# Row-block stores as two transfers of 64 partitions each, in a third-order interaction kernel

## The reference

```python
B, NF, D = 2048, 64, 128          # F: [B, NF, D], W: [NF, NF, D], K_w, Q_w: [D, D], float32
Kf  = einsum('bjd,ed->bje', F, K_w)
S   = einsum('bid,bjd->bij', F, Kf)
out = einsum('bij,ijd->bid', S, W)
out = out + einsum('bid,ed->bie', F, Q_w)
```

## Time and profile before

| what | value |
|---|---|
| median of 3 runs | 606.57 us (606.23 to 607.12) |
| the profiled execution | 606.42 us |
| its span in the trace | 604.6 us |
| TensorE busy | 596.4 us (99%) |
| VectorE busy | 399.2 us (66%) |
| ScalarE busy | 401.5 us (66%) |
| SP's DMA queue (q1) | 20736 packets, 75.83 MB, 31.8% of 16 engines |
| ACT's DMA queue (q10) | 8640 packets, 61.15 MB, 28.4% of 16 engines |
| granted TensorE clock, mean | 0.998 |

### The profile page before, as it was taken

How to read it: one execution, slowest core, us unless ns; L and a number is a source line. 1 busy time by engine, 2 the same in 40 slices (tenths; PEclk the granted TensorE clock), 3 DMA queues, 4 the chain that set the end, 5 groups by cost and what they waited for, 6 DMA issues and landing times.

```text
span 604.6 us, 17904 instructions
## 1 busy us (share of the span) xinstructions
PE 596.4 (99%) x7690; PEld 526.3 (87%) x7690; DVE 399.2 (66%) x412; ACT 401.5 (66%) x696; POOL 0.2 (0%) x4
## 2 busy tenths in 40 slices
PE   9999999999999999999999999999999999999995
PEld 7888989889898898988989898898988989889895
DVE  6556768567685675947749475685756768567486
ACT  7888393874938659295692947939387493865920
POOL 0000000000000000000000000000000000000000
PEclk9999999999999999999999999999999999999999
DMA  8644847457575575755657566484754857557177
GB/s 338 262 141 160 330 165 282 183 185 305 191 281 172 210 266 208 279 196 210 242 192 287 203 238 249 143 319 174 277 209 173 318 179 284 173 209 273 70 281 279
DMA packets 29452, 138.12 MB, mean 228 GB/s; under 512 B 3264, under 2 KB 3776, under 8 KB 21312
## 3 DMA queue, kind: packets, MB, share of 16 engines
q1 hardware_dynamic: 20736, 75.83, 31.8%
q10 hardware_dynamic: 8640, 61.15, 28.4%
HBM read 69.86 MB, written 67.11 MB: 227 GB/s over the span
## 4 chain that ended last, share of the span: by engine, by line
PE 98%; DVE 1%; issue 1%; DVEq 0%
PE ps L509 20%; PE ps L447 20%; PE ps L449 19%; PE ps L448 19%; PE ps L541 18%; DVE o_sb L372 1%; PE ps L576 1%; DVEq L49 0%; DVE o_sb L382 0%; PE ps L467 0%; PE ps L465 0%; PE ps L469 0%; DVE f_hi L388 0%; DVEq L115 0%
## 5 line engine op out<-in xcount | busy, mean ns | idle before, releaser
L337 DVE TENSOR_TENSOR f_lo<-f_ring,f_hi 128x1024 fp32r<-128x1024 f32 x124 | 151.8, 1224 | 168.2 <-ACT f_hi L217 166.6
L231 ACT ACTIVATE q_out<-ps 128x512 f32<-128x512 f32 x256 | 156.9, 613 | 6.6 <-PE ps L449 0.2
L222 ACT ACTIVATE kf<-ps 128x512 f32<-128x512 f32 x256 | 155.8, 609 | 3.5
L372 DVE TENSOR_TENSOR o_sb<-ps,q_out 128x1024 f32<-128x1024 f32 x127 | 145.1, 1215 | 19.4 <-PE ps L541 19.3
L240 ACT ACTIVATE s_t<-ps 128x512 f32<-128x512 f32 x32 | 19.1, 598 | 175.8 <-PE ps L509 175.8
L509 PE MATMUL ps<-f_ring,kf 128*64 128x64 f32 x4096 | 123.5, 222 | 0.3 <-issue 0.3
L509 PEld LDWEIGHTS ps<-f_ring,kf 128*64 128x64 f32 x4096 | 121.1, 138 | 2.6 <-issue 0.8
L541 PEld LDWEIGHTS ps<-s_t,w_sb 64*128 64x128 f32 x2048 | 115.6, 188 | 5.6 <-issue 5.6
L541 PE MATMUL ps<-s_t,w_sb 64*128 64x128 f32 x2048 | 118.6, 274 | 0.0
L447 PE MATMUL ps<-f_hi,k_hi 128*128 128x512 f32 x255 | 101.0, 396 | 0.0
L447 PE MATMUL ps<-f_hi,q_hi 128*128 128x512 f32 x256 | 100.0, 391 | 0.0
(11 more groups left out here) (39 smaller groups left out, 160.3 us busy)
## 6 DMA issues: line engine op xcount, KB each, us to landing
out<-o_sb SPq DMA_DIRECT2D x127, 512.0 KB, 3.5
f_ring<-f_t ACTq DMA_DIRECT2D x58, 1024.0 KB, 4.8
f_ring<-f_t SPq DMA_DIRECT2D x4, 1024.0 KB, 10.6
f_ring<-f SPq DMA_DIRECT2D x8, 256.0 KB, 5.3
w_sb<-w SPq DMA_DIRECT2D x1, 2048.0 KB, 17.8
out<-o_sb SPq DMA_DIRECT2D x2, 256.0 KB, 2.6
o_sb<-first SPq DMA_DIRECT2D x1, 192.0 KB, 2.9
o_sb<-first ACTq DMA_DIRECT2D x1, 192.0 KB, 3.4
```

What stands on the lines that cost most here:

```text
L222: nc.scalar.activation(kf[:, c // 2, c % 2 * CK:(c % 2 + 1) * CK, :, :].rearrange("d k h i -> d (k h i)"), ps[:, 2 * c % 8, :], COPY).then ...
L231: nc.scalar.activation(q_out[:, t % 2, :, :].rearrange("d i (h b) -> d i h b", h=2)[:, :, :, at:at + CK], q_bank(t * CHUNKS + c).rearrange ...
L337: nc.vector.tensor_tensor(f_lo[:, v % SPLIT, :], f_unit(v), f_hi[:, v % SPLIT, :].bitcast(F32), ALU.subtract).then_inc(flo_done, 1)
L372: nc.vector.tensor_tensor(o_sb[:, n % OBUF, :, :, :].rearrange("d x s b -> d s x b"), ps[:, bank:bank + 2, :].rearrange("d s (x b) -> d s ...
```

## The change

Each store of tiles 0 to 14 is issued as two DMAs, the first of partitions 0 to 63 and the second of partitions 64 to 127, one behind the other on SP's queue. The rows keep their 4 KB. Both raise the same semaphore by 16, so a slot's count rises by 32 for each such store, and the new function `stored(slot, n)` gives the count that all the slot's stores before n have brought; the three places that wait on `o_stored` use it. The stores of the last tile are as they were.

```diff
+        def stored(slot, n):
+            last = (TILES - 1) * UNITS
+            return sum(16 if b >= last else 32 for b in range(slot, n, OBUF))
...
             def store(t, k):
                 n = t * UNITS + k
                 sp.wait_ge(out_done, n + 1)
-                sp.dma_start(out[t, k, :, :],
-                             o_sb[:, n % OBUF, :, :, :].rearrange("d x s b -> d (x s b)")).then_inc(o_stored[n % OBUF], 16)
+                src = o_sb[:, n % OBUF, :, :, :].rearrange("d x s b -> d (x s b)")
+                if t == TILES - 1:
+                    sp.dma_start(out[t, k, :, :], src).then_inc(o_stored[n % OBUF], 16)
+                    return
+
+                for part in (slice(0, D // 2), slice(D // 2, D)):
+                    sp.dma_start(out[t, k, part, :], src[part, :]).then_inc(o_stored[n % OBUF], 16)
...
             for n in range(OBUF):
-                uses = len(range(n, TILES * UNITS, OBUF)) + (1 if n == slot else 0)
-                sp.wait_ge(o_stored[n], 16 * uses)
+                sp.wait_ge(o_stored[n], stored(n, TILES * UNITS) + (16 if n == slot else 0))
...
-                again = 1 if n - OBUF == (TILES - 1) * UNITS else 0
-                wait(dve, o_stored[n % OBUF], (n // OBUF + again) * 16)
+                again = 16 if n - OBUF == (TILES - 1) * UNITS else 0
+                wait(dve, o_stored[n % OBUF], stored(n % OBUF, n) + again)
...
-            dve.wait_ge(o_stored[n % OBUF], n // OBUF * 16)
+            dve.wait_ge(o_stored[n % OBUF], stored(n % OBUF, n))
```

## The result

The changed kernel takes 613.36 us in the median of six runs (611.62 to 618.0), the kernel before 606.73 us, now in six runs too (606.03 to 607.28). The ratio is 1.0113, 95% interval 1.0096 to 1.013: slower by 1.1%, near the forecast of 612.8 and inside its range. The runs now spread over 6 us where those of before spread over one.

What follows compares the result with a forecast made beforehand. TensorE, busy 99% of the span, was taken to bound the kernel, the DMA engines its end; 2.1 us of tile stalls plus 4.3 at the end, 6.4 on 606.4, gave 612.8 us, range 606.0 to 620.0.

Steps and rivals of the forecast that it cites:

- The deciding term: Stores of tiles 0 to 14: 16 engines share the way into 64 partitions, so a packet takes up to twice as long.
- The bounds 1.31 and 2.62: Time of a store on all 16 engines in us: 1.31 if unchanged, 2.62 if two engines on one way halve the pace.
- The pace T: Time one 512 KB store takes of all 16 DMA engines: 1.31 us before, 2.55 us forecast after the change.
- partners that fall out of step: Engines sharing a way but reading different halves don't slow each other; this kept the forecast at 2.55, just below 2.62.
- the formula 3T - 7.5: Stall per tile when late sum 7 delays chunk 2 of the projection: sum 2.3 us late against 2.2 slack, from T = 2.5 up.
- 14 waits of 0.15: TensorE's waits ahead of chunk 2 in the projections behind the stores of tiles 0 to 13, 2.1 us in all.
- 8T - 16.1: Delay of the kernel's end as tile 14's longer burst pushes back tile 15's stores: 4.3 us at T = 2.55.
- SP's issues: 120 more DMA instructions of 332 ns on SP; two per store, 0.66 us, fit within 1.14 us between sums: cost 0.
- More packets: 160 packets per store instead of 144, one closing packet more per engine: 0.05 us taken, 0 to 0.16 bounds, hidden.
- The loads: Load issued at 294.3 beside the longer store burst lands 2.6 us later; cast 1.3 us late, cost 0, 1.6 us left.
- the 9 us that I had named: Sign of being wrong: the load at 294.3 landing over 9 us after its issue.
- the prediction's reason against a faster kernel: Rival of a gain by another packet order: no wait on the page could be taken away; chance 0.03.

Runs made afterwards that it cites:

- The stores alone: Kernels without loads and compute issuing only the 128 stores from a constant tile: whole 175.66 us, halves 254.54, even and odd 177.25, both transfers from partitions 0 to 63 339.01.
- its move: Changed kernel with 32 more empty waits on TensorE in tile 1's projection: 620.11 us; gap moved from behind matmul 146 to behind 138 or 137.
- four issues: Changed kernel with each store of tiles 0 to 14 as four transfers of every fourth partition: 637.16 us, ratio 1.0514.

## Why the prediction was right, and where it was not

**The direction and its cause: shown.** The deciding term was where the rows are read from. Stores that read only partitions 0 to 63 take twice as long (2.56 us against 1.29), and even and odd partitions undo it. That pairs of engines share one way in is the reading that fits; no row shows which engine uses which way. The bounds 1.31 and 2.62 were the right ones. The Trainium skill's rule ("SBUF — State Buffer", "Door 1: The DMA port swizzle"), that partitions 0 to 63 reach only half of the ports, agrees with these runs: 205 GB/s from one half, 406 from all. The Trainium skill's statement on the same page ("Can I just issue two DMAs to hit both halves?") that two such transfers gain only 6% doesn't hold for a queue that alternates: 276 against 205 GB/s, a gain of 35%.

**The pace T: mis-sized.** I took 2.55, near the upper bound. The stores alone have 1.90, the burst in the kernel about 1.8 to 1.9 after a start at 191 GB/s, which is T = 2.7. The reason that I gave for staying below 2.62, partners that fall out of step, would be far stronger than I allowed. In the burst's first 1.5 us a 4 KB packet takes 311 ns in the median, afterwards 159, as before the change. That most packets are back at full pace is shown; that it is because their partners are in the other half is argued, from the kernel whose two halves are the same and which stays at 205.

**The tile: mechanism right, price wrong, and a second mechanism missed.** By the formula 3T - 7.5 a T of 1.90 stalls nothing. Yet at the start of the burst, where the stores stand that sums 6 and 7 wait for, the pace is 2.7, and sum 7 came 1.2 to 2.7 us late (3.2 in the first tile), for 2.3 forecast. Where it was 2.65 or more, chunk 2 waited, in four projections, 0.5 us each. These 1.9 us are near the 2.1 that I had as 14 waits of 0.15, by luck. What I had missed is TensorE's own instructions. They come as 16 KB packets through the same DMA engines; I had read that packet only as something that delays stores, and not asked who waits for the packet. In the changed kernel it starts up to 1.1 us later in the stage than the 1.5 us of before, and the gap follows. Over tiles 1 to 14 the scores stages are 6.7 us longer than before, and the projections from tile 1 on 3.8, together 10.5 of the 11.6 us of that execution; I had 2.1. Of what the 14 scores stages last above 7.62, 6.0 us lie in the ten with a late restart, and 1.5 in the four others, mostly in waits for sums; the kernel before had 0.8 of such excess. That the gap is a matter of the instruction stream is shown by its move. That a late packet is its cause rests on the 41 restarts that keep their distance from the packet's end; it leaves little room for another cause, but no run changed the packet alone.

**The end: right formula, wrong T.** 8T - 16.1 with 1.9 is below zero, and the end was not delayed to speak of: from the start of tile 14's rows to the end it takes 31.5 us (584.66 to 616.2) against 31.0, and these 0.5 us are the late restart in the last scores. The stretches show the engines at 0.38 in the microsecond from 603, so tile 14's burst is over just ahead of tile 15's first store:

```profile
591.00:603.00 12.00, 11.66 (x302) 10.79 (x299) 7.77 (x11) 5.78 (x11) 0.00 (x0) 1.00 0.85 280
603.00:604.00 1.00, 1.00 (x23) 1.00 (x21) 0.98 (x3) 0.00 (x0) 0.00 (x0) 1.00 0.38 135
```

I had 4.3 us there. **So the sum was right by luck, by two errors that offset each other**: 4.3 too much at the end, and too little in the tiles. A further 0.6 us of the profiled execution lie in the first projection, ahead of any store, and are no work of the change.

**SP's issues: mis-sized, and the cover was not there.** 332 ns is the price of an issue over 128 partitions that stands alone. Over half of them the first of a tile as a rule takes 466 to 472 ns, though it follows nothing, and one behind another some 600; split by columns, over 128 partitions, the first takes 332 and the second about 450. So both the transfer's form and the one before it count. With even and odd partitions two issues and what lies between them take 1.28 us in an undisturbed row, against a sum each 1.14, and a tile's 16 issues spread over 10 to 12 us instead of the 7.9 of before. It cost nothing because a store takes the engines 1.31 us anyway, not because SP had time; four issues went beyond that. In the changed kernel the median is 780 ns, as SP is held up by the slower stores.

**More packets: hidden, as said.** 403 against 406 GB/s in the stores alone: a closing packet more on each engine costs 0.01 us a store at most.

**The loads: put at nothing, and they cost some 2 us.** In tile 6 the delay was near the forecast and the slack held: the load issued at 300.3 lands after 7.8 us instead of 4.7, 3.1 us later where I had 2.6, VectorE's cast waits 1.75 us, and TensorE doesn't wait. But the loads issued at 72.8 and 111.1 land only after 9.7 and 9.4 us, beyond the 9 us that I had named for tile 6 as a sign of being wrong, and chunk 8 behind them starts 0.5 and 0.8 us late. It is 0.3 us late in two more projections. The rest of the casts' 49 us of waits cost TensorE nothing.

## What to carry to other kernels

A store over half of the partitions should take every other partition, not the lower or the upper half: the rate was 403 against 205 to 276 GB/s. No run here has such a load. When DMA traffic is made slower or longer, ask what else goes through the DMA engines at that moment, the instructions of a busy engine among it, before looking at the waits that the program itself has written. And price an issue by one of the same form that follows another, not by one that stands alone.

## What the runs showed of the hardware

Two things I had not expected. First, a gap in TensorE without any wait of the program, at a fixed place of its instruction stream, in the stages where a 16 KB instruction packet comes late (2.1 us or more behind the start of the scores, instead of 1.5) through DMA engines that are full of store packets. The kernel before has it too, once, with a gap of 0.27 us; the prediction's reason against a faster kernel, that no wait was there to be taken away, had overlooked it:

```profile
100.98 4.53 PE L509 MATMUL ps<-f_ring,kf 128*64 128x64 f32 x146
105.78 0.39 PE L509 MATMUL ps<-f_ring,kf 128*64 128x64 f32 x7 [0.27 <-issue]
```

Second, even and odd transfers are faster than whole ones, by 0.2%. The profile says where: the kernel before needs 37.2, 37.5, 37.1 and 37.1 us in tiles 0, 1, 2 and 5 (from rows to rows), and 36.97 in the others (tile 13 has a shorter projection behind it); with even and odd partitions every tile takes 36.97, in both profiles, 1.0 us in all. In the scores at 100.78 of that kernel the instruction packet starts 0.9 us behind the stage's start, and the stage has no gap:

```profile
100.78 7.68 PE L519 MATMUL ps<-f_ring,kf 128*64 128x64 f32 x256
```

where before it came at 103.4, 2.4 us behind the start at 100.98. The stores of a tile are issued over 10 to 12 us in this kernel and over 7.9 in the one before, so fewer packets can stand ahead of the instructions'. That is the likely reason; it was not tested.
